# Requests for a pair's operands placed after the row of maxima and between the quarter refreshes on SyncE; one transfer for both copies' rows; the width table through a skewed view

## The chip, the cores and the metric

The kernel runs on one core of a Trainium2 chip. Its time is the device time of one execution in microseconds (us); the median of the runs is what counts.

## What is computed

Eight images of 32 x 32 tokens with 96 channels go through three residual blocks. Cut to what matters here:

```python
# layer 0: 6 heads of 16; rel_h, rel_w come from q and two tables of relative positions
attn = einsum('bqd,bkd->bqk', q * SCALE, k)
attn = attn.reshape(b*NH, h, w, h, w) + rel_h[:, :, :, :, None] + rel_w[:, :, :, None, :]
x = x + (softmax(attn.reshape(b*NH, hw, hw)) @ v -> heads joined) @ proj_w + proj_b     # input normed in groups
# layer 1: causal attention, 6 heads of 16
t = t + (softmax(where(causal, q @ k^T / 4, min)) @ v -> heads joined) @ w_proj          # input layer-normed
# feed-forward: 4 experts, the best 2 of each token weighted
t = t + sum over e of gate[e] * (gelu(LN(t) @ w1[e] + b1[e]) @ w2[e] + b2[e])
```

## The kernel before, in words

Five engines and the DMA queues run programs that are written out by hand; their order is the order of the code, and semaphores tie them together (`upto` gives the count that a stage of an item has to reach). An item is one image. The loop body is `attention(it, 1)` (layer 1 of item `it`), `attention(it, 0)` (layer 0 of the item after it) and `mix` (the experts of `it`, between them the norms and projections that the next item needs).

Each attention has three steps p = 0, 1, 2, one for a pair of heads, and each step runs over eight key tiles kt and the two heads hh of the pair. TensorE writes transposed scores to psT (L687 in layer 0, L690 in layer 1), ScalarE takes the exponential to probs (L1087), TensorE multiplies with the values (L709, L717). A row of negated maxima, one per query, is an extra row of the query operand, so it has to be there before the first scores of a pair. While pair p runs, TensorE computes plain scores for pair p + 1 (`max_scores`, L658) and VectorE reduces them (`maxima`, L1401); at kt = 6 the maxima are transposed (`transpose_max`, L668), ScalarE negates them (`neg_max`, L1042) and itself issues the transfer that lays them out as a row (L1048): `qr<-negb` in layer 1, `qs<-negr` in layer 0, where two copies of the query operand need it, so there are two transfers of 8 KB. In step p = 2 of layer 1 the same is done for pair 0 of the next layer 0 (called "lead").

The layer-0 operands of a pair are qs (128 rows, copies c = 0, 1) and ks, in slot p % 2. They are read back from DRAM by `load_pair(p)`, 17 transfers on SyncE's queue: for each copy two of 256 KB, two quarters of 64 KB and three of 128 KB, then three of 128 KB for ks: 2,432 KB in all. Only 8 of the 32 rows of relative height lie in a copy at a time (a quarter, for two key tiles): copy 0 has quarter 0 for kt 0 and 1 and gets quarter 2 for kt 4 and 5; copy 1 quarter 1, then quarter 3. ScalarE issues this refresh (L1085, two transfers of 64 KB) when it comes to the exponential of (kt = 1, hh = 1) or (kt = 3, hh = 1); TensorE waits for it at kt = 4 and 6 (`turn_in`). Before L1048 ScalarE waits in layer 0 for the whole pair (`pair_in`), since the row lies among the loaded rows.

SyncE's order: at the start of layer 1 `load_x`, then `first_pairs`, which is `load_pair(0)` and `load_pair(1)` of the next layer 0; then after each pair `gather` (eight transfers of 32 KB, when ScalarE has written `ot`). In layer 0: the token load x0 (L536), `load_pair(2)` when the scores of pair 0 are done (L482 on), `gather(0)`, `spill_levels` (query and key levels of the next item to DRAM, wait, and `qr` read back), `gather(1)`, `spill_wide` and its wait, `operands0` (qa, ka), `gather(2)`, then the slots of layer 1.

At the start of the program VectorE builds the table of relative widths with 32 instructions (L1312), then the other constants, then works on the relative terms (`rel_high` on ScalarE L1121, `rel_low` on VectorE L1530). `rel_high` waits at its first turn until all spills of queries and keys are in DRAM.

Of the kernel before, what the change touches and what calls it, by code (L numbers as in the profile page):

```python
# [15 lines left out]
NH, HD = 6, 16  # L16
# [104 lines left out]
def by_act(what):  # L121
# [37 lines left out]
    "negmax_in": {"attn1": 16 * (PAIRS - 1), "lead": 32, "attn0": 32 * (PAIRS - 1), "next_mix": 16},  # L159
# [98 lines left out]
def build(nc, x_tok, x_t, consts, hots, masks, w_qkv0, b_qkv0, w_p0, b_p0, rel_h, rel_w, w_qkv1, w_p1, gate_w, gate_b,  # L258
          w1, b1, w2, b2, out):
    with ExitStack() as ctx:  # L260
# [99 lines left out]
        mrow = sb("mrow", [P, 2, 2 * NT])  # L360
        negm = [sb("negr", [2 * NT, 2, P], F32R), sb("negb", [2 * NT, 2, P], BF16)]
# [13 lines left out]
        relr_w = probs[0:C, 1, :].rearrange("c (a b) -> c a b", a=WS)  # L375

# [38 lines left out]
        n_setup, n_ones = 28, 8  # L415
# [10 lines left out]
        def _(sp):  # L426
# [50 lines left out]

            def load_pair(p):

                heads, slot, done = slice(2 * p, 2 * p + 2), p % 2, pair_in[p % 2]  # L480
                for c in range(2):
                    sp.dma_start(qs_raw[W_HI:W_HI + WS, slot, c], scr_rel[R_W_HI:R_W_HI + WS, heads]).then_inc(done, 16)  # L482
                    sp.dma_start(qs_raw[W_LO:W_LO + WS, slot, c], scr_rel[R_W_LO:R_W_LO + WS, heads]).then_inc(done, 16)
                    for dst, src in quarter_rows(p, c, c):
                        sp.dma_start(dst, src).then_inc(done, 16)
                    for n, (q, _) in enumerate(S_PARTS):
                        a = QK_ROWS + n * HD
                        sp.dma_start(qs_raw[a:a + HD, slot, c], scr32_d[:, q, heads]).then_inc(done, 16)
                for n, (_, k) in enumerate(S_PARTS):
                    a = QK_ROWS + n * HD  # L490
                    sp.dma_start(ks_raw[a:a + HD, slot], scr32_d[:, k, heads]).then_inc(done, 16)
# [7 lines left out]
            def first_pairs(it, st):  # L499
# [3 lines left out]
                load_pair(0)  # L503
                load_pair(1)
# [19 lines left out]
            def attention1(it):  # L524
# [36 lines left out]
            spill_levels(None, "p_qkv0")  # L561
            spill_wide(None, "p_qkv0")
            operands0()
            relative(None, "p_rel")
            first_pairs(None, "p_rel")
# [18 lines left out]
        def _(pe):  # L584
# [79 lines left out]
            def transpose_max(it, layer, p):  # L664
# [3 lines left out]
                mm(psM[0:2 * NT, 0:P], mrow[:, p % 2, :], ident, is_transpose=True, start=True,  # L668
                   stop=True).then_inc(m_full, 1)

            def attention(it, layer):
# [55 lines left out]
                for p in range(PAIRS):  # L727
# [19 lines left out]

                    if layer == 0:
                        pe.wait_ge(negmax_in, upto("negmax_in", it, st, 32 * p))
                        pe.wait_ge(pair_in[p % 2], upto(("pair_a_in", "pair_b_in")[p % 2], it, st, PAIR_LOADS * (p // 2 + 1)))  # L750
                    else:
                        pe.wait_ge(negmax_in, upto("negmax_in", it, st, 16 * p))
# [168 lines left out]
            def first_rows(it, st):  # L921
# [5 lines left out]
                mm(o[0:2 * NT, 0:P], mrow[:, 0, :], ident, is_transpose=True, start=True, stop=True).then_inc(t_full, 1)  # L927
# [65 lines left out]
        def _(act):  # L993
# [44 lines left out]
            def neg_max(it, layer, p):  # L1038
# [3 lines left out]
                A(negm[layer][:, p % 2, :], psM[0:2 * NT, 0:P], ACT.Copy, scale=-1.0).then_inc(m_free, 1)  # L1042
# [19 lines left out]
            def attention(it, layer):  # L1062
# [232 lines left out]
        def _(dve):  # L1295
# [9 lines left out]
            def constants():  # L1305
# [368 lines left out]
```

## Time and profile before

| | |
|---|---|
| median of 3 runs | 2129.08 us (2126.45 to 2130.79) |
| profiled execution: its time, its span | 2129.47 us, 2127.6 us |
| granted TensorE clock, mean over the span | 0.915 of full speed |
| TensorE matmul, weight load | 1741.9 us (82%), 694.9 us (33%) |
| VectorE, ScalarE, GpSimd | 1222.2 us (57%), 1073.3 us (50%), 294.8 us (14%) |
| SP's queue (q1), ACT's queue (q10) | 180.18 MB, 6.79 MB |

TensorE is the busiest engine, but its share is an average over stages; what matters is what ends its idle times and at which point of an item they stand. Item 4 (layer 1 from 1012 us, layer 0 from 1092 us, mix from about 1182 us) is taken as the example below. Times in a timeline count from the start of the span. A bracket at the end of a timeline row is the idle time of the engine just before it and what ended it.

### The profile page before, as it was taken

The page shows a single profiled execution, that of the slowest core. Times are in us where ns is not written, and L with a number is a line of the kernel's source. Part 1 is how long each engine was busy: PE and PEld are TensorE (multiplying, and loading weights), DVE is VectorE, ACT ScalarE, POOL GpSimd, SP SyncE. Part 2 cuts the span into 40 slices and gives each one's busy share as a digit, 9 for nine tenths or more (in the row PEclk, how much of TensorE's full clock was granted, in tenths as well). Part 3 has the DMA queues.
Part 4 walks back from the last instruction along what each step waited for, and adds up shares of the span by engine and source line. Part 5 has one row for each costly group of instructions (what it writes and reads, how often), then busy time and mean ns, then how long its engine had stood idle before and what let it go on. Part 6 is the DMA issues. An engine that isn't in the chain of part 4 may idle for free.

```text
span 2127.6 us, 25037 instructions
## 1 busy us (share of the span) xinstructions
PE 1741.9 (82%) x8928; PEld 694.9 (33%) x8928; DVE 1222.2 (57%) x2526; ACT 1073.3 (50%) x1375; POOL 294.8 (14%) x191
## 2 busy tenths in 40 slices
PE   1578478898799968998798987999789987989858
PEld 0122222343233433343233432334322432324333
DVE  7753657446664657636674465646576365743631
ACT  0246335574456724575355743567345753566433
POOL 5112101301023100501023010321005010200000
PEclk7589579999899989999899998999899998999979
DMA  6756371636427291555606374372816446141200
GB/s 142 140 90 127 68 166 24 103 70 160 83 54 130 52 182 26 104 84 126 114 23 116 57 175 71 62 127 55 181 24 101 80 127 107 24 68 46 39 11 8
DMA packets 73744, 188.57 MB, mean 89 GB/s; under 512 B 23188, under 2 KB 24853, under 8 KB 66964
## 3 DMA queue, kind: packets, MB, share of 16 engines
q1 hardware_dynamic: 69780, 180.18, 44.3%
q10 hardware_dynamic: 3840, 6.79, 1.3%
q8 instruction: 71, 1.16, 0.3%
q14 instruction: 53, 0.43, 0.1%
HBM read 115.62 MB, written 58.20 MB: 82 GB/s over the span
## 4 chain that ended last, share of the span: by engine, by line
PE 53%; DVE 20%; DMA 12%; ACT 7%; issue 4%; SPq 2%; ACTq 1%; DVEq 0%
PE psS L658 11%; DVE mx L1401 8%; PE psOM L709 6%; PE psT L832 6%; PE psT L687 5%; PE psOM L717 5%; PE psS L846 5%; DMA qr<-negb 4%; PE psT L690 4%; DMA qs<-scr_rel 4%; DVE mrow L1503 3%; DMA qs<-negr 2%; DVE qs L1530 2%; ACT probs L1087 2%; PE psT L608 2%
## 5 line engine op out<-in xcount | busy, mean ns | idle before, releaser
L1087 ACT ACTIVATE probs<-psT 128x1024 f32<-128x1024 f32 (+7 forms) x768 | 623.6, 837 | 585.4 <-PE psT L687 250.8
L1401 DVE TENSOR_REDUCE mx<-psS 128x1 f32<-128x512 f32 (+3 forms) x1152 | 681.5, 640 | 390.4 <-PE psS L658 253.4
L687 PE MATMUL psT<-qs,ks 128*128 128x512 f32 x768 | 341.1, 515 | 44.0 <-DMA qs<-negr 16.0
L658 PE MATMUL psS<-ka,qa 128*128 128x512 bf16 x768 | 305.4, 407 | 45.1 <-DVE mx L1401 26.2
L690 PE MATMUL psT<-qr,kr 97*128 97x512 bf16 (+3 forms) x576 | 194.8, 367 | 64.8 <-DMA qr<-negb 63.8
L709 PE MATMUL psOM<-probs,v 128*32 128x512 f32 x1536 | 224.8, 608 | 11.6 <-ACT probs L1087 11.6
L832 PE MATMUL psT<-xf,w1s 97*128 97x512 f32 x384 | 187.4, 622 | 1.8 <-DVE mrow L1503 1.8
L658 PEld LDWEIGHTS psS<-ka,qa 128*128 128x128 bf16 x768 | 71.8, 97 | 344.4 <-DVE mx L1401 281.3
L687 PEld LDWEIGHTS psT<-qs,ks 128*128 128x128 f32 x768 | 141.0, 197 | 125.4 <-ACT probs L1087 48.0
L846 PE MATMUL psS<-probs,w2s 128*96 128x512 f32 x384 | 180.7, 596 | 0.8 <-ACT att L1146 0.8
L1530 DVE TENSOR_TENSOR qs<-psOM,qs 32x768 fp32r<-32x768 f32 x128 | 121.8, 952 | 95.2 <-ACT qs L1121 93.4
L717 PE MATMUL psOM<-probs,v 128*32 128x384 f32 (+3 forms) x1440 | 150.5, 444 | 20.4 <-ACT probs L1087 20.4
L658 PE MATMUL psS<-kr,qr 96*128 96x512 bf16 (+3 forms) x384 | 142.7, 384 | 22.9 <-DVE mx L1401 19.4
L1138 ACT ACTIVATE probs<-psT 128x1024 f32<-128x1024 f32 x96 | 98.3, 1024 | 115.8 <-PE psT L832 115.2
L1261 POOL TENSOR_TENSOR lb<-lb,il 96x1024 f32<-96x1024 f32 x7 | 16.6, 2371 | 785.3 <-ACT il L1111 785.3
L1503 DVE TENSOR_REDUCE mrow<-psT 128x1 f32<-128x128 f32 (+7 forms) x128 | 91.4, 753 | 46.9 <-PE psT L880 45.9
L1215 POOL TENSOR_TENSOR split<-au,split 96x1024 bf16<-96x1024 f32 x8 | 17.0, 2130 | 622.9 <-ACT split L1036 622.9
L832 PEld LDWEIGHTS psT<-xf,w1s 97*128 97x128 f32 x384 | 72.2, 197 | 85.3 <-issue 75.4
L690 PEld LDWEIGHTS psT<-qr,kr 97*128 97x128 bf16 x576 | 62.2, 108 | 101.0 <-DMA qr<-negb 68.4
L1512 DVE SCALAR_TENSOR_TENSOR x<-psOM,g,x 128x96 f32<-128x96 f32 x256 | 60.4, 308 | 60.0 <-PE psOM L864 60.0
L692 PE MATMUL psT<-mask_k,ident_b 128*128 128x128 bf16 x384 | 85.3, 232 | 0.0
L846 PEld LDWEIGHTS psS<-probs,w2s 128*96 128x96 f32 x384 | 58.1, 163 | 81.9 <-issue 72.8
(162 smaller groups left out, 1718.7 us busy)
## 6 DMA issues: line engine op xcount, KB each, us to landing
scr_rel<-qs SPq DMA_DIRECT2D x16, 1536.0 KB, 13.1
qs<-scr_rel SPq DMA_DIRECT2D x96, 256.0 KB
qs<-scr SPq DMA_DIRECT2D x144, 128.0 KB
scr<-split SPq DMA_DIRECT2D x24, 576.0 KB, 4.7
qr<-scr SPq DMA_DIRECT2D x48, 192.0 KB, 6.6
scr<-kr SPq DMA_DIRECT2D x24, 384.0 KB, 5.2
ks<-scr SPq DMA_DIRECT2D x72, 128.0 KB
qa<-scr SPq DMA_DIRECT2D x32, 192.0 KB, 5.4
```

The source lines that it names most:

```text
L658: last = mm(bank[:, 0:n], q[0:rows, h, t * P:(t + 1) * P], k[0:rows, h, kc * HALF:kc * HALF + n], start=True, stop=not diagonal)
L687: last = mm(o[:, a:b], ks[:, p % 2, hh, keys], qs[:, p % 2, kt // 2 % 2, hh, a:b], start=True, stop=True)
L690: last = mm(o[:, a:b], kr[:, h, keys], qr[:, h, a:b], start=True, stop=a != q0)
L709: last = mm(psO[j:j + 2 * HD, :], v[:, kt, p, hh * HD:(hh + 2) * HD], probs[:, (2 * kt + hh) % 4, c * HALF:(c + 1) * HALF], start=kt == 0, ...
L717: last = mm(psO[j:j + 2 * HD, first * P:HALF], v[:, kt, p, hh * HD:(hh + 2) * HD], every[:, c, first:], start=kt == 0, stop=kt == NT - NC + c)
L832: last = mm(o[:, c * HALF:(c + 1) * HALF], w1s[:, a:a + P], xf[:, c * HALF:(c + 1) * HALF], start=True, stop=True)
L846: last = mm(psS[0:C, c, :], w2s[:, n, :], hbuf[:, n % 4, c * HALF:(c + 1) * HALF], start=j == 0, stop=j == HJ - 1)
L1087: A(probs[:, n % 4, q0:T], psT[:, t_slot(ts, m), q0:T], ACT.Exp).then_inc(t_free, 1)
L1138: A(hbuf[:, n % 4, :], psT[:, t_slot(stage, fill), :], ACT.Gelu).then_inc(ta_free, 1)
L1401: V.reduce_max(mx[layer][:, p % 2, (h % 2) * NT + t, kc:kc + 1], psS[:, s_bank(st, fill), 0:max_cols(layer, t, kc)], AX).then_inc(s_free, 1)
L1503: V.reduce_max(mrow[:, 0, n:n + 1], psT[:, t_slot(st, fill), 0:cols], AX).then_inc(t_free, 1)
L1530: ins = V.tensor_tensor(rest[0], rest[1], lead[0].bitcast(F32), ALU.subtract)
```

## The change

- `first_pairs` is split: its waits (`spilled`) stay at the start of layer 1, the loads go. `load_pair(0)` now follows `gather(1, 0)` and a wait for the row of pair 1, `load_pair(1)` follows `gather(1, 1)` and a wait for the row of pair 2. In the prologue the order stays.
- `load_pair` is made of `load_copy(p, 0)`, `load_copy(p, 1)` and `load_keys(p)`. In layer 0, pair 2 is asked for in these parts: copy 0 when the scores of pair 0 are done, the keys and copy 1 during pair 1, after the one and the other refresh.
- The refreshes go from ScalarE's queue to SyncE's (`turn_quarter`, with a wait for the same scores).
- `spill_levels` is split: its waits and the reading back of qr (`levels_back`) now come after the refreshes of pair 2; `gather(0, 2)` comes ahead of `operands0`.
- Both copies' rows of maxima go in one transfer of 16 KB: the maxima are written twice side by side, 32 columns are transposed instead of 16.
- The table of widths: one broadcast copy (96 x 32 x 63) and one subtraction (96 x 32 x 32) through a view whose rows start one element further back each time.

```diff
+            def levels_back(it, st):
+
                 sp.wait_ge(spill_q, upto("spill_q", it, st, 16))
                 sp.wait_ge(spill_k, upto("spill_k", it, st, 16))
                 fill_slots(qr, scr_d, 0, Q_SLOTS, slice(0, NH), qr_in)
...
+            def turn_quarter(it, p, c):
+
+                st, n = att_t(0, (p * NT + 2 * c + 1) * 2 + 1)
+                sp.wait_ge(t_full, upto("t_full", it, st, n + 1))
+                for dst, src in quarter_rows(p, c, c + 2):
+                    sp.dma_start(dst, src).then_inc(turn_in[c], 16)
...
                 if next_lead(it):
-                    first_pairs(it - 1 if it else None, "mix")
+                    spilled(it - 1 if it else None, "mix")
                 for p in range(PAIRS):
                     gather(it, 1, p)
+                    if p + 1 < PAIRS and next_lead(it):
+                        sp.wait_ge(negmax_in, upto("negmax_in", it, "attn1", 16 * (p + 1)))
+                        load_pair(p)
 
             def attention0(it, row):
 
                 sp.wait_ge(t_free, upto("t_free", it, "attn0", 0))
                 sp.dma_start(x0[:, :, :], x_tok[row]).then_inc(x0_in, 16)
+                turn_quarter(it, 0, 0)
+                turn_quarter(it, 0, 1)
                 st, n = att_t(0, 2 * NT - 1)
                 sp.wait_ge(t_full, upto("t_full", it, st, n + 1))
-                load_pair(2)
+                load_copy(2, 0)
                 gather(it, 0, 0)
+                turn_quarter(it, 1, 0)
+                load_keys(2)
+                turn_quarter(it, 1, 1)
+                load_copy(2, 1)
                 if next_layer0(it):
                     spill_levels(it, "qkv0")
                 gather(it, 0, 1)
+                turn_quarter(it, 2, 0)
+                turn_quarter(it, 2, 1)
                 if next_layer0(it):
+                    levels_back(it, "qkv0")
                     sp.wait_ge(pair_in[0], upto("pair_a_in", it, "attn0", 2 * PAIR_LOADS))
                     spill_wide(it, "qkv0")
+                gather(it, 0, 2)
                 if next_layer0(it):
                     operands0()
-                gather(it, 0, 2)
...
-                rows = [qr[C:C + 1, 2 * p:2 * p + 2, :]] if layer else [qs_raw[MAX_ROW:MAX_ROW + 1, p % 2, c] for c in range(2)]
-                for row in rows:
-                    act.dma_start(row.rearrange("o h (t q) -> o (h t) q", q=P),
-                                  negm_raw[layer][:, p % 2, :]).then_inc(negmax_in, 16)
+                if layer:
+                    row = qr[C:C + 1, 2 * p:2 * p + 2, :].rearrange("o h (t q) -> o (h t) q", q=P)
+                else:
+                    row = qs_raw[MAX_ROW:MAX_ROW + 1, p % 2].rearrange("o c h (t q) -> o (c h t) q", q=P)
+                act.dma_start(row, negm_raw[layer][:, p % 2, :]).then_inc(negmax_in, 16)
...
-                            if layer == 0 and hh == 1 and kt in (1, 3):
-                                for dst, src in quarter_rows(p, kt // 2, kt // 2 + 2):
-                                    act.dma_start(dst, src).then_inc(turn_in[kt // 2], 16)
...
-                for r in range(WS):
-                    last = WIN - 1 - r
-                    ins = V.tensor_scalar(relr_w[:, r, :], relf_w[:, WS - 1 - r:last + 1], relf_w[:, last:last + 1], None,
-                                          ALU.subtract)
-                ready(ins)
+                ready(V.tensor_copy(straight, relf_w.unsqueeze(1).to_broadcast([C, WS, WIN])))
+                ready(V.tensor_tensor(relr_w, skewed, skewed[:, :, WS - 1:WS].to_broadcast([C, WS, WS]), ALU.subtract))
```

## Rows read from the trace of the kernel before

**Rows 1.** The page's part 4: the chain that ended last, by engine
```profile
PE 53%; DVE 20%; DMA 12%; ACT 7%; issue 4%; SPq 2%; ACTq 1%; DVEq 0%
```

**Rows 2.** The waits of PE, whole span: us in total, times, longest us
```profile
PE psT L690 <- DMA qr<-negb: 63.8, 16, 9.8
...
PE psT L687 <- DMA qs<-scr_rel: 12.4, 7, 3.0
```

**Rows 3.** Who waited for L1048 (us, times); then PE's waits in item 7's layer 1
```profile
  PE psT L690: 61.9, 15
...
PE psT L690 <- DMA qr<-negb: 0.2, 1, 0.2
```

**Rows 4.** Timeline, layer 1 of item 4, pair 0: SP's first load, ACT's row, TensorE's wait
```profile
1014.12 0.42 SPq L482 DMA_DIRECT2D qs<-scr_rel  x1
...
1032.83 0.52 ACTq L1048 DMA_DIRECT2D qr<-negb  x1
...
1042.04 0.61 PE L690 MATMUL psT<-qr,kr 97*128 97x512 bf16 x1 [7.69 <-DMA qr<-negb]
```

**Rows 5.** Busy time by window: length, PE, PEld, DVE, ACT, POOL, clock, DMA share, GB/s
```profile
1014.00:1042.00 28.00, 19.23 (x135) 7.80 (x133) 13.94 (x30) 10.11 (x17) 0.00 (x0) 0.81 1.04 188
...
1042.00:1050.00 8.00, 7.96 (x33) 3.82 (x37) 4.99 (x12) 4.37 (x5) 0.00 (x0) 0.50 0.46 82
...
1052.00:1060.00 8.00, 7.08 (x49) 2.48 (x47) 6.10 (x13) 3.78 (x7) 0.00 (x0) 1.00 0.03 7
```

**Rows 6.** Timeline, layer 1 of item 4, pair 2, to the first scores of layer 0
```profile
1070.73 0.39 PE L690 MATMUL psT<-qr,kr 97*128 97x512 bf16 x1 [0.24 <-DMA qr<-negb]
...
1073.90 0.51 SPq L449 DMA_DIRECT2D au<-ot  x1
...
1089.66 1.16 ACTq L1048 DMA_DIRECT2D qs<-negr  x2
...
1092.17 0.49 PE L687 MATMUL psT<-qs,ks 128*128 128x512 f32 x1 [0.34 <-DMA qs<-negr]
```

**Rows 7.** Chain that ended last, prologue: the first row of layer 0 (start, us, what)
```profile
105.59 11.11 DMA qs<-negr
```

**Rows 8.** Timeline, layer 0 of item 4, end of pair 0 to end of pair 1
```profile
1118.86 0.32 SPq L482 DMA_DIRECT2D qs<-scr_rel  x1
...
1131.29 0.65 ACTq L1085 DMA_DIRECT2D qs<-scr_rel  x2
...
1139.13 0.62 ACTq L1085 DMA_DIRECT2D qs<-scr_rel  x2
...
1142.56 0.50 PE L687 MATMUL psT<-qs,ks 128*128 128x512 f32 x1 [1.78 <-DMA qs<-scr_rel]
...
1154.17 1.16 ACTq L1048 DMA_DIRECT2D qs<-negr  x2
```

**Rows 9.** Timeline, layer 0 of item 4, pair 2: gather, refresh, scores of kt 4
```profile
1161.62 0.51 SPq L449 DMA_DIRECT2D au<-ot  x1
...
1166.53 0.59 SPq L450 DMA_DIRECT2D lb<-ot  x1
...
1168.33 1.65 ACTq L1085 DMA_DIRECT2D qs<-scr_rel  x2
...
1169.44 0.70 PE L687 MATMUL psT<-qs,ks 128*128 128x512 f32 x2 [0.34 <-ACT probs L1087]
1171.10 0.73 PE L687 MATMUL psT<-qs,ks 128*128 128x512 f32 x2 [0.95 <-ACT probs L1087]
```

**Rows 10.** Timeline of the prologue; last, a group by line (count, busy us, mean ns)
```profile
19.70 18.85 DVE L1312 TENSOR_SCALAR probs<-lb 96x32 f32<-96x32 f32 x32 [5.79 <-DMA il<-hots]
...
48.05 1.73 SPq L439 DMA_DIRECT2D qa<-scr  x4
...
57.88 0.80 ACT L1121 ACTIVATE qs<-psOM 32x768 fp32r<-32x768 f32 x1 [0.74 <-PE psOM L633]
...
L1412 DVE TENSOR_TENSOR lb<-lb,il 96x1024 f32<-96x1024 f32 x9 | 11.0, 1222 | 76.9 <-ACT il L1111 76.9
```

More of the change, by code:

```diff
@@ L158 @@
     "rowmax": {"attn1": PAIRS - 1, "lead": 1, "attn0": PAIRS - 1},
-    "negmax_in": {"attn1": 16 * (PAIRS - 1), "lead": 32, "attn0": 32 * (PAIRS - 1), "next_mix": 16},
+    "negmax_in": {"attn1": 16 * (PAIRS - 1), "lead": 16, "attn0": 16 * (PAIRS - 1), "next_mix": 16},
     "p_used": {s: ATT_FILLS for s in _ATT},
@@ L359, in build @@
         mx = [sb(f"mx{l}", [P, 2, 2 * NT, NC]) for l in (0, 1)]
-        mrow = sb("mrow", [P, 2, 2 * NT])
-        negm = [sb("negr", [2 * NT, 2, P], F32R), sb("negb", [2 * NT, 2, P], BF16)]
+        mrow = sb("mrow", [P, 2, 2, 2 * NT])
+        negm = [sb("negr", [4 * NT, 2, P], F32R), sb("negb", [2 * NT, 2, P], BF16)]
         negm_raw = [negm[0][:, :, :].bitcast(F32), negm[1]]
@@ L375, in build @@
         relr_w = probs[0:C, 1, :].rearrange("c (a b) -> c a b", a=WS)
+        copies = probs[0:C, 2:4, :].rearrange("c s t -> c (s t)")
+        straight = copies.rearrange("c (a b) -> c a b", b=WIN + 1)[:, :, 0:WIN]
+        skewed = copies[:, WS - 1:WS - 1 + WS * WIN].rearrange("c (a b) -> c a b", b=WIN)[:, :, 0:WS]
         gs6 = sb("gs6", [C, 2, 6])
@@ L414, in build @@
         first_loads = [(cst[:, :], consts), (wqkv[0][0:C, :], w_qkv0), (wqkv[0][C:C + 1, :], b_qkv0)]
-        n_setup, n_ones = 28, 8
+        n_setup, n_ones = 29, 8
         def quarter_rows(p, c, n):
@@ L476, in operands0, with load_copy, load_keys, load_pair @@
                 fill_slots(ka, scr_d, 1, K_SLOTS[:4], slice(0, NH), ab_in)
-            def load_pair(p):
+            def load_copy(p, c):
                 heads, slot, done = slice(2 * p, 2 * p + 2), p % 2, pair_in[p % 2]
[L481 to L488, printed above, removed]
+                sp.dma_start(qs_raw[W_HI:W_HI + WS, slot, c], scr_rel[R_W_HI:R_W_HI + WS, heads]).then_inc(done, 16)
+                sp.dma_start(qs_raw[W_LO:W_LO + WS, slot, c], scr_rel[R_W_LO:R_W_LO + WS, heads]).then_inc(done, 16)
+                for dst, src in quarter_rows(p, c, c):
+                    sp.dma_start(dst, src).then_inc(done, 16)
+                for n, (q, _) in enumerate(S_PARTS):
+                    a = QK_ROWS + n * HD
+                    sp.dma_start(qs_raw[a:a + HD, slot, c], scr32_d[:, q, heads]).then_inc(done, 16)
+            def load_keys(p):
                 for n, (_, k) in enumerate(S_PARTS):
                     a = QK_ROWS + n * HD
-                    sp.dma_start(ks_raw[a:a + HD, slot], scr32_d[:, k, heads]).then_inc(done, 16)
+                    sp.dma_start(ks_raw[a:a + HD, p % 2], scr32_d[:, k, 2 * p:2 * p + 2]).then_inc(pair_in[p % 2], 16)
+            def load_pair(p):
+                load_copy(p, 0)
+                load_copy(p, 1)
+                load_keys(p)
+            def turn_quarter(it, p, c):
[3 more added lines that the diff above has]
+                    sp.dma_start(dst, src).then_inc(turn_in[c], 16)
             def relative(it, st):
@@ L497, in relative, with spilled @@
                 sp.dma_start(scr_rel[:, 3:NH], rel_raw[:, 3:NH]).then_inc(spill_rel, 16)
-            def first_pairs(it, st):
+            def spilled(it, st):
                 sp.wait_ge(spill_rel, upto("spill_rel", it, st, 32))
                 sp.wait_ge(rel_lead_bf, upto("rel_lead_bf", it, st, NH))
-                load_pair(0)
-                load_pair(1)
             def slots1(it):
@@ L561, in _ @@
             spill_levels(None, "p_qkv0")
+            levels_back(None, "p_qkv0")
             spill_wide(None, "p_qkv0")
@@ L564, in _ @@
             relative(None, "p_rel")
-            first_pairs(None, "p_rel")
+            spilled(None, "p_rel")
+            load_pair(0)
+            load_pair(1)
             attention0(None, 0)
@@ L667, in transpose_max @@
                 pe.wait_ge(m_free, upto("m_free", it, ms, n))
-                mm(psM[0:2 * NT, 0:P], mrow[:, p % 2, :], ident, is_transpose=True, start=True,
+                rows = (4 - 2 * layer) * NT
+                mm(psM[0:rows, 0:P], mrow[:, p % 2].rearrange("p c r -> p (c r)")[:, 0:rows], ident, is_transpose=True, start=True,
                    stop=True).then_inc(m_full, 1)
@@ L746, in between @@
                         sent[0] = until
+                    pe.wait_ge(negmax_in, upto("negmax_in", it, st, 16 * p))
                     if layer == 0:
-                        pe.wait_ge(negmax_in, upto("negmax_in", it, st, 32 * p))
                         pe.wait_ge(pair_in[p % 2], upto(("pair_a_in", "pair_b_in")[p % 2], it, st, PAIR_LOADS * (p // 2 + 1)))
-                    else:
-                        pe.wait_ge(negmax_in, upto("negmax_in", it, st, 16 * p))
                     for kt in range(NT):
@@ L926, in first_rows @@
                 o = take_mixed(it, st, ("tmax", 0))
-                mm(o[0:2 * NT, 0:P], mrow[:, 0, :], ident, is_transpose=True, start=True, stop=True).then_inc(t_full, 1)
+                mm(o[0:2 * NT, 0:P], mrow[:, 0, 0, :], ident, is_transpose=True, start=True, stop=True).then_inc(t_full, 1)
             def group_means(it, st):
@@ L1041, in neg_max @@
                 act.wait_ge(negmax_in, upto("negmax_in", it, ms, 16 * max(p - 2, 0) if layer else 0))
-                A(negm[layer][:, p % 2, :], psM[0:2 * NT, 0:P], ACT.Copy, scale=-1.0).then_inc(m_free, 1)
+                A(negm[layer][:, p % 2, :], psM[0:(4 - 2 * layer) * NT, 0:P], ACT.Copy, scale=-1.0).then_inc(m_free, 1)
                 act.wait_ge(m_free, upto("m_free", it, ms, n + 1))
@@ L1405, in maxima @@
                         dve.wait_ge(m_full, upto("m_full", it, st, max(p - 1 - layer, 0)))
-                        V.tensor_tensor(mrow[:, p % 2, :], mx[layer][:, p % 2, :, 0], mx[layer][:, p % 2, :, 1],
-                                        ALU.max).then_inc(rowmax, 1)
+                        left, right = (mx[layer][:, p % 2, :, c].unsqueeze(1).to_broadcast([P, 2, 2 * NT]) for c in range(NC))
+                        V.tensor_tensor(mrow[:, p % 2], left, right, ALU.max).then_inc(rowmax, 1)
             def den(it, st):
@@ L1502, in first_maxima @@
                 dve.wait_ge(t_full, upto("t_full", it, st, fill + 1))
[L1503 removed]
+                V.reduce_max(mrow[:, 0, 0, n:n + 1], psT[:, t_slot(st, fill), 0:cols], AX).then_inc(t_free, 1)
             def expert_add(it, stage, x):
```

1 line of the change is left out of this document (removed).

## The prediction

> **What bounds the kernel now.** I read the chain that ended last first: TensorE carries 53% of it and transfers 12% [rows 1], so here it is worth asking which transfers TensorE sits and waits for. The waits of TensorE answer it: 63.8 us in 16 waits for `qr<-negb`, the row of maxima in layer 1, and 12.4 us in 7 waits for `qs<-scr_rel`, the quarter refresh of layer 0 [rows 2]. While TensorE waits at such a point nothing else goes on: VectorE's maxima and ScalarE's exponentials are fed by it. The reader should then separate long waits from short ones. The row issued at L1048 was waited for 15 times, 61.9 us together; the last item, which loads no pairs for a next one, waits 0.2 us [rows 3]. So the long ones are seven, one for each item with a next layer 0.
>
> The timeline shows why. SyncE asks for pairs 0 and 1 of the next layer 0 from 1014.12 on; ScalarE asks for the row at 1032.83; TensorE gets it at 1042.04 after 7.69 us of idleness [rows 4]. Up to that moment the transfer engines are busy without a gap (share 1.04, 188 GB/s), and afterwards they run on at 0.46 for some 8 us [rows 5]. The row stands behind 4.9 MB that nobody needs for 50 us. TensorE pays twice: for the next 8 us its granted clock is 0.50, the lower level (1.2 GHz), after it had stood idle, and in the window from 1052 it is 1.00 again [rows 5].
>
> **The change, step by step.** The sum is made against the profiled execution, 2129.5 us (span 2127.6, the rest lies around it); the median, 2129.1, is 0.4 us lower.
>
> *1. Row of pair 1 in layer 1.* The loads move behind it, so its queue is empty but for the store and `load_x`, asked for 18 us earlier. 15 waits of 61.9 us, eight of them short (0.24 us, as the one at 1070.73 [rows 6]; 8 x 0.24 = 1.9): seven long ones make 60.0 us. They shrink to 0.24 each: 60.0 - 1.7 = **-58.3**.
>
> *2. The clock after it.* In the 8 us at half clock VectorE did 4.99 us of work, in 8 us at full clock 6.10 [rows 5]. The same 4.99 would take 4.99 / 6.10 x 8 = 6.5 us: 1.5 us a stall, 10.5 for seven if all are like this one, 0 if VectorE sets the pace anyway. I take **-8**.
>
> *3. What is late next: the row of the lead pair.* `load_pair(1)` now goes out in pair 2 of layer 1, behind `gather(1, 1)`. Count from the start of that pair, 1070.73: the gather starts 3.2 us later and its eight issues take 5, so the load is asked for from +8.2. The row is asked for at +18.9 and used at +21.4 (1092.17) [rows 6]. A pair is 2,432 KB; at 188 GB/s that is 13.2 us, so the queue is full until +21.4, at the very time at which the row landed before. If the row passes, the cost is 0; if it waits for the whole queue and half of the 8 us tail that two pairs had [rows 5], it lands at about +26, 4.6 us late. I take 2 us, since the row of rows 4 came in when the full stretch ended and not after the tail: 7 x 2 = **+14** (0 to +32). The same for `load_pair(0)` and the row of pair 2: asked for from about +8 in a pair that lasts 28.7 us (1042.04 to 1070.73), it is through by +23, before the row goes out: 0 (to +4). The new wait of SyncE for the row of the next pair stands behind a gather that itself waits for that pair's first exponentials, so it is over when SyncE comes to it; `gather(1, 2)` and x0 queue behind, with 13 us to spare.
>
> *4. One transfer instead of two.* ScalarE spends 1.16 us on the two rows (1154.17 [rows 8]), one takes 0.52 [rows 4]: 0.64 us ahead of the last exponentials of a pair, on which TensorE's last values and the next pair wait. 16 such ends of pairs 0 and 1 in eight layers 0: **-10** (0 to -10). The lead row is in step 3. The wider transpose and reduction add columns to instructions that stand 40 times; nothing.
>
> *5. Refresh in pair 1 of layer 0.* Pair 2 is asked for at 1118.86, the refresh at 1131.29 behind it, and TensorE gets it at 1142.56, 1.78 us too late [rows 8]. Now only copy 0 (1,024 KB, 5.4 us at 188 GB/s) and a gather lie ahead of it; SyncE comes to it when the gather is issued, about 1131, so the refresh keeps its time of issue and lands 6 us before it is needed. The 12.4 us of [rows 2] go: **-12** (-8 to -18 with the clock). The cover of the moved part: copy 1 is now asked for after the refresh of 1139.13 and ScalarE needs it at 1154.17, less 3 us that the stage gets shorter [rows 8]: 11 us for 5.4 us of data. Behind copy 1 stand the spills (3 to 8 us later than before; TensorE first needs the read-back qr in the mix).
>
> *6. Refresh in pair 2.* Off ScalarE: at 1168.33 its issue takes 1.65 us beside SyncE's, and TensorE then waits 0.34 and 0.95 us for exponentials [rows 9]: -1 us in seven layers, -7 (0 to -9). On SyncE it stands behind `gather(0, 1)`, which goes from 1161.62 to 1167.1; two issues of 0.3 us and some 2 us of landing (the second lead row took 1.9 from 1090.3) put it at 1169.2 to 1169.8, and TensorE wants it at 1169.1 [rows 6, 9]. I take 0.5 us late, 8 x 0.5 = +4 (0 to +20 with a gather that starts later). Together **-3**. `levels_back` and `spill_wide` move behind it by some 5 us; `gather(0, 2)` waits for its own pair until 1182, which hides that.
>
> *7. The table.* 18.85 us of VectorE become one copy of 2016 and one subtraction of 1024 elements a row; 1024 elements took 1.22 us, so under 4 us [rows 10]. But ScalarE's first `rel_high` (57.88) also waits for the spills, and SyncE, which waits for the same, went on at 48.05 [rows 10]. The 15 us become 57.88 - 48.05 = **-10** (-8 to -10).
>
> Sum: -58.3 - 8 + 14 - 10 - 12 - 3 - 10 = -87.3; 2129.5 - 87.3 = 2042.2, on the median's footing about **2042 us**.
>
> **Rivals.**
> *The lead row passes.* Transfers on ScalarE's queue could be served between those of SyncE's. For it: by +18.9 all of `load_pair(1)` has been issued for 3 us, and what is left is mostly tail. Against it: rows 4, where the row was asked for 3 us after the last load and still took 9 us. Step 3 becomes 0: 2042 - 14 = 2028. The Trainium skill states such a rule ("DMA: Bandwidth & Descriptors", section "Queues, rings and completion order": each transfer engine goes round its queues packet by packet); by it the row of rows 4 should not have waited at all, so the trace speaks against it, and by it the sum would be the 2028 just worked out.
>
> *The wait only moves.* In the prologue the lead row is asked for behind two pairs and takes 11.11 us [rows 7] where it takes 1.9 in item 4: 9.2 us more. If one pair ahead does the same, step 3 is 7 x 9.2 = 64 instead of 14, and the clock falls there instead (step 2 gone): 2042 + 50 + 8 = 2100. Against it: half the bytes, asked for 11 us earlier.
>
> *The refresh of pair 2 is late by 2.5 us*, because SyncE is held in the gather: step 6 is +13 instead of -3: 2058.
>
> *Slower: ScalarE stuck behind copy 1.* ScalarE runs in order, and before the row of pair 2 it waits for all of the pair. What was asked for at 1131.29 behind pair 2 was usable at 1142.56, 23.7 us after the pair's first request [rows 8]. If copy 1, asked for at 1139.8, took as long, it would land 12.7 us after the 11 us it has; exponentials, values and the next pair stand still, in eight layers: +102, 2144. It turns the sign from 22 us of landing on (87 / 8 = 11 on top of the 11). Against it: 1 MB on a queue that is empty by then.
>
> *The row's wait has another cause* than the loads: steps 1, 2 and 3 fall away: 2042 + 52 = 2094. Item 7 speaks against it [rows 3].
>
> **How the numbers follow.** Forecast 0.47, lead row passes 0.22, late refresh 0.13, wait moves 0.12, stuck ScalarE 0.04, other cause 0.02. With the bounds of the steps the forecast itself runs from about 2018 to 2075. The range 2010 to 2085 takes in the first three with their bounds and leaves out the other 0.18. A measurement of this kernel can tell about 0.2% (4 us) from no change; only the stuck ScalarE lies on the slower side: slower 0.04, within 0.2% 0.02, faster 0.94.
>
> **What would show it.** Step 1: TensorE's waits for `qr<-negb` down from 63.8 to about 5 us. Step 2: the clock at 1.00 through the first 8 us of pair 1. Step 3: waits for `qs<-negr` at the start of layer 0, 2 us each, `load_pair(1)` issued 8 us into pair 2. Step 5: no wait for `qs<-scr_rel` in pair 1. Step 6: a wait for it at kt 4 of pair 2 of at most 1 us. Step 7: `rel_high` starting at 48. The forecast is wrong if the lead row waits 5 us or more, or if ScalarE stands before L1048 in pair 1 of layer 0.

## The result, and the profile after

The changed kernel takes 2110.3 us (median of 8 runs, 2106.1 to 2117.1) where the kernel before took 2128.2 us (median of 8 as well): a ratio of 0.9919, 95% interval 0.9900 to 0.9937. It is faster, as forecast, but by 18 us instead of 87, and 2110 lies above the range. What came is the rival that had 0.12: the wait moved to the lead pair's row. Lines have moved: L687 is now L722, L690 is L725, L658 is L692, L1048 is L1083, L1085 is L512 (on SyncE), L482 is L487, L1087 is L1118.

The page's chain by engine, after, against [rows 1]:

```profile
PE 56%; DVE 21%; DMA 9%; ACT 6%; issue 4%; SPq 3%; another core or an unknown queue 2%; ACTq 0%; DVEq 0%
```

Transfers fell from 12 to 9% of the chain, no more. (The 2% of an unknown queue stand where 61 of L692's 768 matmul records are missing from this trace.) TensorE's waits for transfers, after, against [rows 2] (us in total, times, longest):

```profile
PE psT L722 <- DMA qs<-negr: 65.7, 8, 14.2
...
PE psT L725 <- DMA qr<-negb: 20.7, 16, 4.2
...
PE psT L722 <- DMA qs<-scr_rel: 17.2, 8, 3.2
```

The row of layer 1 went from 63.8 to 20.7 us. But the row of layer 0 takes 65.7 us in 8 waits, one of them the prologue's 14.2, so (65.7 - 14.2) / 7 = 7.4 us in each item. Before, that row stood in the same view as:

```profile
PE psT L687 <- DMA qs<-negr: 16.0, 11, 12.6
```

The sums of both rows are 86.4 us after and 79.8 us before (63.8 and 16.0).

Where the time went shows best stage by stage. A stage here runs from the timeline's start of one pair's first score matmul to that of the next pair; the means are over the seven items that have a next layer 0, in us. The last line runs from the first to the last score matmul of the pair only. The kernels e1 to g1 are the experiments below. Each column is one profiled execution.

```
stage               before  after    e4    e1    e2    f3    e3    f1    g1
layer 1, pair 0      27.18  18.85 27.42 18.91 18.80 18.64 18.65 18.79 27.02
layer 1, pair 1      27.76  27.40 28.03 28.00 27.71 28.34 27.76 25.45 27.63
layer 1, pair 2      21.43  29.53 21.16 22.58 23.01 26.00 30.12 21.18 21.16
layer 0, pair 0      29.67  30.10 28.84 34.58 28.58 30.05 30.03 29.00 29.22
layer 0, pair 1      34.52  31.45 31.44 32.88 31.43 31.46 31.50 31.45 35.03
layer 0, pair 2      20.06  21.53 22.01 21.68 21.62 21.05 19.59 19.60 20.24
```

Pair 0 of layer 1 gave 8.33 x 7 = 58.3 us and pair 2 took 8.10 x 7 = 56.7 of them back. What the kernel kept is pair 1 of layer 0, 3.07 x 7 = 21.5 us. By the six lines together the seven items gained 12.3 us of the 18.6 by which the two spans (2127.6 and 2109.0) differ; the rest lies outside them, in the mixes and at the program's start.

The item of [rows 4 to 9], timeline after, from pair 2 of layer 1 to the first scores of layer 0 (a bracket is the idle time before, and what ended it):

```profile
1056.81 0.61 PE L725 MATMUL psT<-qr,kr 97*128 97x512 bf16 x1 [1.67 <-DMA qr<-negb]
...
1066.32 1.83 SPq L487 DMA_DIRECT2D qs<-scr_rel  x1
...
1073.58 1.36 SPq L499 DMA_DIRECT2D ks<-scr  x3
...
1077.03 0.51 ACTq L1083 DMA_DIRECT2D qs<-negr  x1
...
1079.40 0.51 SPq L452 DMA_DIRECT2D au<-ot  x1
...
1084.38 0.58 SPq L558 DMA_DIRECT2D x<-x_tok  x1
...
1087.68 1.67 PE L722 MATMUL psT<-qs,ks 128*128 128x512 f32 x2 [8.94 <-DMA qs<-negr]
```

`load_pair(1)` goes out from 1066.32, the lead row at 1077.03, and TensorE has it 10.6 us later, after 8.94 us of idleness. Busy time by window of the same stretch, after (columns as in [rows 5]: length, PE, PEld, DVE, ACT, POOL, clock, DMA share, GB/s):

```profile
1070.00:1075.00 5.00, 4.18 (x31) 1.28 (x29) 4.66 (x8) 2.18 (x4) 0.00 (x0) 1.00 1.03 152
1075.00:1080.00 5.00, 2.95 (x34) 1.29 (x30) 1.19 (x3) 2.08 (x6) 0.00 (x0) 1.00 1.05 184
1080.00:1085.00 5.00, 0.00 (x0) 0.00 (x0) 0.00 (x0) 0.00 (x0) 0.00 (x0) 0.56 0.88 113
1085.00:1088.00 3.00, 0.32 (x1) 0.29 (x1) 0.00 (x0) 0.00 (x0) 0.00 (x0) 0.50 0.92 156
1088.00:1092.00 4.00, 3.81 (x9) 1.38 (x9) 2.66 (x5) 1.94 (x2) 0.00 (x0) 0.64 0.09 29
```

The transfer engines are at 0.88 to 1.05 of their time until TensorE has its row, and from 1080 to 1085 no compute engine does anything. The granted clock falls to the lower level in the idle time, and it is still below the upper one when layer 0 begins: what [rows 5] showed at the start of pair 1 now stands here.

### The profile page after: what moved, and what is told of

It reads as the page before. It is cut to its first block, busy times and chain, and to the rows that moved or that the text cites. A ratio compares the mean times of both kernels' runs of the same rounds, so it can differ in the third digit from the quotient of the medians.

```text
span 2109.0 us, 24922 instructions
## 1 busy us (share of the span) xinstructions
PE 1729.6 (82%) x8867; PEld 693.9 (33%) x8928; DVE 1221.8 (58%) x2496; ACT 1071.8 (51%) x1375; POOL 298.9 (14%) x191
## 4 chain that ended last, share of the span: by engine, by line
PE 56%; DVE 21%; DMA 9%; ACT 6%; issue 4%; SPq 3%; another core or an unknown queue 2%; ACTq 0%; DVEq 0%
PE psS L692 12%; DVE mx L1429 9%; PE psOM L744 7%; PE psT L722 6%; PE psT L865 5%; PE psOM L752 5%; PE psS L879 4%; PE psT L725 4%; DMA qs<-negr 4%; DVE mrow L1531 3%; DVE qs L1558 2%; PE psT L642 2%; DMA qr<-negb 2%; DVE x L1540 1%
## 5 line engine op out<-in xcount | busy, mean ns | idle before, releaser
L1118 ACT ACTIVATE probs<-psT 128x1024 f32<-128x1024 f32 (+7 forms) x768 | 622.5, 836 | 578.0 <-PE psT L722 299.9
L722 PE MATMUL psT<-qs,ks 128*128 128x512 f32 x768 | 351.8, 533 | 90.8 <-DMA qs<-negr 65.7
L692 PE MATMUL psS<-ka,qa 128*128 128x512 bf16 x707 | 292.7, 421 | 36.3 <-DVE mx L1429 16.7
L725 PE MATMUL psT<-qr,kr 97*128 97x512 bf16 (+3 forms) x576 | 194.3, 366 | 23.0 <-DMA qr<-negb 20.7
L722 PEld LDWEIGHTS psT<-qs,ks 128*128 128x128 f32 x768 | 147.1, 205 | 170.3 <-DMA qs<-negr 67.9
L692 PEld LDWEIGHTS psS<-ka,qa 128*128 128x128 bf16 x768 | 74.3, 100 | 347.9 <-DVE mx L1429 281.9
L865 PE MATMUL psT<-xf,w1s 97*128 97x512 f32 x384 | 182.2, 607 | 1.8 <-DVE mrow L1531 1.8
L692 PE MATMUL psS<-kr,qr 96*128 96x512 bf16 (+3 forms) x384 | 135.1, 363 | 25.1 <-DVE mx L1429 20.8
L910 PE MATMUL psT<-kr,qr 96*128 96x512 bf16 (+1 forms) x192 | 53.5, 352 | 35.4 <-DVE mrow L1531 14.8
## 6 DMA issues: line engine op xcount, KB each, us to landing
scr<-kr SPq DMA_DIRECT2D x24, 384.0 KB, 11.5
```

The costliest lines, as they stand in the source:

```text
L692: last = mm(bank[:, 0:n], q[0:rows, h, t * P:(t + 1) * P], k[0:rows, h, kc * HALF:kc * HALF + n], start=True, stop=not diagonal)
L722: last = mm(o[:, a:b], ks[:, p % 2, hh, keys], qs[:, p % 2, kt // 2 % 2, hh, a:b], start=True, stop=True)
L725: last = mm(o[:, a:b], kr[:, h, keys], qr[:, h, a:b], start=True, stop=a != q0)
L865: last = mm(o[:, c * HALF:(c + 1) * HALF], w1s[:, a:a + P], xf[:, c * HALF:(c + 1) * HALF], start=True, stop=True)
L1118: A(probs[:, n % 4, q0:T], psT[:, t_slot(ts, m), q0:T], ACT.Exp).then_inc(t_free, 1)
```

## Experiments

**e4: the loads back where they were.** All of the change but its first part.

```diff
                     spilled(it - 1 if it else None, "mix")
+                    load_pair(0)
+                    load_pair(1)
                 for p in range(PAIRS):
                     gather(it, 1, p)
-                    if p + 1 < PAIRS and next_lead(it):
-                        sp.wait_ge(negmax_in, upto("negmax_in", it, "attn1", 16 * (p + 1)))
-                        load_pair(p)
```

> The changed kernel with both pairs' loads put back to the start of layer 1 as before; all else of the change stays. Theory: moving the loads only moved the wait from the row of pair 1 (pair 0 back to 27 us) to the lead row (pair 2 back to 21.4 us), so it was worth next to nothing, and this kernel takes 2105 to 2115, as the changed one; what the change gained is in pair 1 of layer 0 (some 3 us an item) and in the prologue. Rival: the move of the loads gained what the change gained, and the rest nothing: then this kernel takes about 2128.

2107.2 us, ratio 0.9909 (0.9877 to 0.9941), not to be told from the changed kernel. The move of the loads, the part with the largest term, is worth nothing as it was made; TensorE's wait for `qr<-negb` is back, and that for `qs<-negr` is down to (16.9 - 12.2) / 7 = 0.7 us an item outside the prologue:

```profile
PE psT L724 <- DMA qr<-negb: 64.2, 17, 10.0
...
PE psT L721 <- DMA qs<-negr: 16.9, 8, 12.2
```

**e1: all of pair 1 behind the lead row.** Its three lots go out between the refreshes in pair 0 of layer 0.

```diff
-                    if p + 1 < PAIRS and next_lead(it):
+                    if p == 0 and next_lead(it):
...
                 turn_quarter(it, 0, 0)
+                if it is not None:
+                    load_copy(1, 0)
+                    load_keys(1)
                 turn_quarter(it, 0, 1)
+                if it is not None:
+                    load_copy(1, 1)
```

> The changed kernel, but pair 1 of the next layer 0 is asked for behind the lead row: copy 0 and the keys after the first refresh of layer 0, copy 1 after the second. Theory A, the lead row waits for what SyncE's queue still has to move ahead of it: with nothing ahead, pair 2 of layer 1 goes from some 29.5 us back to the 21.4 it took before, the seven waits of some 7 us for the row go to 0.3; about 50 us less than the changed kernel, 2055 to 2065. Theory B, the single transfer of 32 rows into one partition is itself slow: pair 2 stays at 29 us and the time at 2110. In both, pair 0 of layer 0 may grow by 1 to 3 us if copy 1 comes late for the row of pair 1.

2107.4 us, ratio 0.9898 (0.9859 to 0.9937): Theory A came out for the stage, but not for the time. The lead pair falls from 29.53 to 22.58 us, so it was `load_pair(1)` that the lead row stood behind. But pair 0 of layer 0 rises from 30.10 to 34.58 and pair 1 from 31.45 to 32.88, which takes most of it back. The timeline of e1 there:

```profile
1091.84 0.31 SPq L487 DMA_DIRECT2D qs<-scr_rel  x1
...
1105.83 0.56 ACTq L1088 DMA_DIRECT2D qs<-negr  x1
...
1106.48 1.94 ACT L1123 ACTIVATE probs<-psT 128x1024 f32<-128x1024 f32 x2 [2.94 <-DMA qs<-scr]
1107.56 2.84 PE L749 MATMUL psOM<-probs,v 128*32 128x512 f32 x8 [2.38 <-ACT probs L1123]
...
1111.93 0.49 PE L727 MATMUL psT<-qs,ks 128*128 128x512 f32 x1 [1.53 <-DMA qs<-negr]
```

Copy 1, asked for at 1091.84, is there 14 us later; ScalarE stands 2.94 us ahead of its row, TensorE 2.38 us for the exponentials behind it, and then 1.53 us for the row itself. The wait has moved a third time, and in the form that the prediction had called ScalarE stuck behind copy 1, only one pair earlier.

**e2: half of pair 1 ahead of the lead row.** Copy 0 (1,024 KB) stays in pair 2 of layer 1; keys and copy 1 go out in layer 0, as in e1.

```diff
-                        load_pair(p)
+                        if p == 0:
+                            load_pair(0)
+                        else:
+                            load_copy(1, 0)
...
                 turn_quarter(it, 0, 0)
+                if it is not None:
+                    load_keys(1)
                 turn_quarter(it, 0, 1)
+                if it is not None:
+                    load_copy(1, 1)
```

> The changed kernel, but only copy 0 of pair 1 (1,024 KB of 2,432) is asked for ahead of the lead row, in pair 2 of layer 1; the keys come after the first refresh of layer 0, copy 1 after the second. Theory A (the row waits until the queue ahead of it is through): 1,024 KB are through about 8 us after the request, 3 us before the row is asked for, so pair 2 takes 21.4 to 22 us and the time is that of the kernel with all of it behind, or up to 5 us less. Rival: any load in that pair holds the row up in proportion to its bytes; then pair 2 takes about 25 us and the time is about 2080.

2057.3 us, ratio 0.9676 (0.9636 to 0.9716): some 50 us less than the changed kernel and near to the forecast of 2042. The lead pair takes 23.01 us instead of 29.53, and pair 0 of layer 0 28.58, without the price that e1 paid there. Timeline of e2 at the lead row:

```profile
1051.19 0.51 ACTq L1090 DMA_DIRECT2D qs<-negr  x1
...
1053.44 0.51 PE L729 MATMUL psT<-qs,ks 128*128 128x512 f32 x1 [0.53 <-DMA qs<-negr]
```

With 1,024 KB asked for from 1040.59 on, the row takes 2.2 us; with 2,432 KB it took 10.6. By the trace's records of single pieces of a transfer, the last piece of those 1,024 KB goes 1.2 us before the row is asked for. So the mechanism of the forecast was sound, and its size was not.

**f3: the same requests with two quarters fewer.** Both copies' quarters of pair 1 (four transfers of 8 rows, 256 KB of 2,432) move into layer 0; everything else stays ahead of the lead row. The third argument of `load_copy` says whether the quarters go with it; `load_quarter` asks for them alone.

```diff
-                        load_pair(p)
+                        load_copy(p, 0, p == 0)
+                        load_copy(p, 1, p == 0)
+                        load_keys(p)
...
                 turn_quarter(it, 0, 0)
+                if it is not None:
+                    load_quarter(1, 0)
+                    load_quarter(1, 1)
```

> The changed kernel, but the four quarter transfers of pair 1 (64 KB each, 8 rows each, 256 KB of its 2,432) are asked for in layer 0, after the first refresh, no longer ahead of the lead row. Theory A, the row waits for bytes: 10% less at 150 GB/s is 1.7 us, so pair 2 of layer 1 takes 27.8 us instead of 29.5 and the time falls by some 12 us. Theory B, the 8-row transfers load only half of the transfer engines and it is their longer backlog that holds the second half of the row: then the row comes 3.5 us earlier or more, pair 2 takes 26 us or less and the time falls by 25 us.

2086.7 us, ratio 0.9792 (0.9761 to 0.9824). TensorE's waits in f3:

```profile
PE psT L732 <- DMA qs<-negr: 40.6, 8, 12.6
```

(40.6 - 12.6) / 7 = 4.0 us an item instead of 7.4, and the lead pair is 3.5 us shorter. At some 150 GB/s (the mean of the windows above until the row came), 262,144 bytes are 1.7 us. So these four cost about twice what their bytes do. The Trainium skill ("DMA: Bandwidth & Descriptors", section "Why a DMA increments its semaphore by 16 and not by 1") says that a transfer is spread over the largest number of engines, up to 16, that divides the outer dimension of both its sides; for 8 rows that would be 8 of them. The 3.5 us agree. How the row itself moves agrees too. It goes as 48 small pieces on ScalarE's queue (q10). In the changed kernel half of them move in the window 1081.4:1083, none in 1083:1084.8, and the other half in 1084.8:1086.2; in f3 all 48 move in 1066.5:1069.2 (pieces, MB, share of 16 engines):

```profile
q10 hardware_dynamic: 24, 0.01, 4.7%
...
q10 hardware_dynamic: 24, 0.01, 4.2%
...
q10 hardware_dynamic: 48, 0.02, 5.6%
```

In all seven items of the changed kernel the second half starts 2.5 to 3.5 us after the first, in f3 0.4 to 0.8 us. The records do not name the engine of a piece, and the same bytes in transfers of 16 rows were not run. That it was half of the engines fits, but is not shown.

**e3: the refresh ahead of the gather.** In pair 2 of layer 0.

```diff
-                gather(it, 0, 1)
                 turn_quarter(it, 2, 0)
+                gather(it, 0, 1)
                 turn_quarter(it, 2, 1)
```

> The changed kernel, with one line moved: SyncE issues the first refresh of pair 2 ahead of the gather of pair 1, no longer behind it. Theory: the 17 us of waiting for the refresh in pair 2 (eight waits of about 2 us) come from the 5 us that SyncE spends on the gather; they go to under 3 us together, and the time falls by 8 to 14 us to about 2098. Rival: the refresh is late because its landing is slow or because TensorE has become faster there, not by the place in the queue; then the waits stay at 1.5 us or more each and the time at 2110.

2099.7 us, ratio 0.9880 (0.9843 to 0.9916). Timeline of the changed kernel, pair 2 of layer 0:

```profile
1152.51 0.51 SPq L452 DMA_DIRECT2D au<-ot  x1
...
1153.70 1.67 SPq L452 DMA_DIRECT2D au<-ot  x1
...
1158.58 1.49 SPq L512 DMA_DIRECT2D qs<-scr_rel  x4
...
1162.45 2.02 PE L722 MATMUL psT<-qs,ks 128*128 128x512 f32 x4 [2.46 <-DMA qs<-scr_rel]
```

and of e3:

```profile
1155.19 0.61 SPq L512 DMA_DIRECT2D qs<-scr_rel  x2
1155.85 0.51 SPq L452 DMA_DIRECT2D au<-ot  x1
...
1162.71 1.56 PE L722 MATMUL psT<-qs,ks 128*128 128x512 f32 x4 [0.34 <-ACT probs L1118]
```

Behind the gather the refresh goes out at 1158.58 and TensorE loses 2.46 us; ahead of it the wait is gone, and the scores of the pair take 19.59 instead of 21.53 us: 1.94 x 7 = 13.6 us. The medians differ by 10.6 us as expected, but the intervals of the two ratios overlap.

**e6: the constants after GpSimd.** VectorE waits with the table until GpSimd has done its first spills.

```diff
                 dve.wait_ge(first_in, 16 * len(first_loads))
+                dve.wait_ge(wide3, upto("wide3", None, "p_qkv0", 2))
```

> The changed kernel, but VectorE's constants, the table among them, wait until GpSimd has made the first operand parts. In the changed kernel the first eight of these instructions took 1.8 to 3.0 us each, small ones of 63 columns too, while GpSimd was at work; the same ones took 0.2 to 1.3 us before. Theory A, it is GpSimd's work beside them that stretches them: after it, the small ones take 0.2 to 0.3 us, those of 1024 columns 0.7 to 1.3, the copy of 2016 columns about 2 and the subtraction 1.2; the constants start 16 us later and the relative terms some 2 to 5 us later than in the changed kernel. Theory B, their operands or the view make them slow: the times stay as they were and the relative terms start 15 us later.

2121.7 us in one run. The question was how long the instructions take by themselves. Timeline of the prologue, VectorE and GpSimd, in the changed kernel:

```profile
19.82 1.21 DVE L1341 COPY probs<-lb 96x2016 f32<-96x2016 f32 x1 [5.92 <-DMA il<-hots]
21.07 3.03 DVE L1342 TENSOR_TENSOR probs<-probs 96x1024 f32<-96x1024 f32 x1
...
25.08 2.19 DVE L1345 SCALAR_TENSOR_TENSOR lb<-lb,cst 96x63 f32<-96x63 bf16 x1
...
38.73 6.33 DVE L1351 CAST ka<-au 64x1024 bf16<-64x1024 f32 x6
...
20.03 2.98 POOL L1266 TENSOR_TENSOR xnt<-kr,split 96x1024 f32<-96x1024 f32 x1
23.08 1.92 POOL L1267 CAST split<-xnt 96x1024 bf16<-96x1024 f32 x1
```

and in e6:

```profile
36.91 1.21 DVE L1342 COPY probs<-lb 96x2016 f32<-96x2016 f32 x1 [22.99 <-POOL kr L1276]
38.15 1.22 DVE L1343 TENSOR_TENSOR probs<-probs 96x1024 f32<-96x1024 f32 x1
...
39.64 0.28 DVE L1346 SCALAR_TENSOR_TENSOR lb<-lb,cst 96x63 f32<-96x63 bf16 x1
...
44.58 4.29 DVE L1352 CAST ka<-au 64x1024 bf16<-64x1024 f32 x6
...
20.04 2.12 POOL L1266 TENSOR_TENSOR xnt<-kr,split 96x1024 f32<-96x1024 f32 x1
22.23 1.03 POOL L1267 CAST split<-xnt 96x1024 bf16<-96x1024 f32 x1
```

Alone, the subtraction takes 1.22 us and an addition of 63 elements 0.28; beside GpSimd they take 3.03 and 2.19, and GpSimd's own steps grow from 2.12 to 2.98 and from 1.03 to 1.92. The table's instructions took 4.3 us instead of 18.9. But the eight behind them took 14.6 us where they had taken 5.1, and the casts 6.3 where they had taken 4.3: of 14.6 us saved, 11.5 were spent by instructions that moved up beside GpSimd's work.

**g1: only the one transfer for both rows,** in the kernel before.

```diff
-                rows = [qr[C:C + 1, 2 * p:2 * p + 2, :]] if layer else [qs_raw[MAX_ROW:MAX_ROW + 1, p % 2, c] for c in range(2)]
+                row = qs_raw[MAX_ROW:MAX_ROW + 1, p % 2].rearrange("o c h (t q) -> o (c h t) q", q=P)   # layer 0
```

> The kernel before with one part of the change alone: both copies' rows of maxima go in one transfer (the maxima written twice side by side, 32 columns transposed), everything else as before. Step 4's theory: the 0.64 us of ScalarE ahead of the last exponentials are on the path, so each end of pairs 0 and 1 of layer 0 comes some 0.6 us earlier: pair 1 of layer 0 and pair 0 of layer 0 each 0.6 us shorter, 16 ends, about -10 us, ratio about 0.995. Rival: ScalarE's issue lies beside TensorE's own work, and the wider transpose and reduction cost as much as the saved issue: no stage shorter by more than 0.2 us, ratio within 0.002 of 1; then the 3 us by which pair 1 of layer 0 got shorter in the changed kernel all belong to the refresh (step 5).

2122.0 us, ratio 0.9967 (0.9948 to 0.9986), some 7 us (3 to 11): between the two expectations, with 10 us inside the interval. Its profiled execution, 2130.4 us, is the slowest of its 12 runs, so differences of half a microsecond in its stages prove little. Pair 2 of layer 1 is 0.27 us shorter and pair 0 of layer 0 0.45. Pair 1 of layer 0 is not shorter but 0.5 longer, and TensorE's waits in g1 fit that:

```profile
PE psT L688 <- DMA qs<-scr_rel: 17.3, 8, 3.5
```

against 12.4 us in [rows 2]: TensorE came earlier to a refresh that still stood behind pair 2's load. So the 3.07 us that the changed kernel gains in that pair go with the refresh and its queue; nothing in g1 gives them to the one transfer.

**f1: three lots, every row on an empty queue.** Copy 0 of pair 0 at the start of layer 1; its copy 1 and keys behind the row of pair 1; copy 0 of pair 1 behind the row of pair 2; its keys and copy 1 between the refreshes of layer 0, in the prologue too; and the edit of e3.

```diff
                     spilled(it - 1 if it else None, "mix")
+                    load_copy(0, 0)
                 for p in range(PAIRS):
...
-                        load_pair(p)
+                        if p == 0:
+                            load_copy(0, 1)
+                            load_keys(0)
+                        else:
+                            load_copy(1, 0)
...
                 turn_quarter(it, 0, 0)
+                if it is None:
+                    load_copy(1, 0)
+                load_keys(1)
                 turn_quarter(it, 0, 1)
+                load_copy(1, 1)
```

> The changed kernel with the loads spread so that each row of maxima finds the queue empty: copy 0 of pair 0 at the start of layer 1, copy 1 and keys of pair 0 in pair 1, copy 0 of pair 1 in pair 2, its keys and copy 1 after the first and second refresh of layer 0 (in the prologue all of pair 1 there); the first refresh of pair 2 ahead of the gather. Theory (a row costs what SyncE's queue still holds when it is asked for, 1.4 MB being through in some 11 us after a gather): the waits for the row of pair 2 of layer 1, some 2.8 us each in the kernel with half of pair 1 ahead, go to 0.3 (-18 us), the prologue's 12 us wait to 1 (-11), the refresh's 17 to 2 (-4 to -10): about 2024 from 2057, pair 1 of layer 1 from 27.6 to 25 us. Rival: pair 1 is as long as it is for another reason (VectorE's 32 maxima and the group statistics); then it stays at 27 us and the time is about 2040.

2014.5 us, ratio 0.9458 (0.9424 to 0.9491): faster than both kernels, by 118 us against a kernel before that took 2132.9 on this experiment's chip. Transfers carry 4% of its chain. TensorE's waits in f1:

```profile
PE psT L730 <- DMA qs<-negr: 10.4, 9, 3.2
...
PE psT L733 <- DMA qr<-negb: 5.8, 16, 2.1
```

Both rows together cost 16.2 us where they cost 79.8 before and 86.4 after the change. Pair 1 of layer 1, which hardly moved in any other kernel, falls from 27.40 to 25.45 us: it was still held by the row of pair 2 behind `load_pair(0)`, and the rival, that VectorE paces it, falls. f1 makes several edits at once; the stages tell them apart, and the largest gain is in the lead pair (29.53 to 21.18).

## Why the prediction was wrong

*Step 1, the row of pair 1, was right:* -58.3 forecast, -58.3 measured by the stage (27.18 to 18.85, seven times).

*Step 3 failed, by its size.* It put +14 where +56.7 came. The order of events was as foreseen: the load from 9.5 us into pair 2 (8.2 forecast), the row asked for at 20.2 (18.9). What it had wrong is how long the load holds the row: it let 2,432 KB through in 13.2 us and added 2 us. The trace's records of single pieces tell the load's apart by their size (4,096 and 8,192 bytes). From first to last they take 15.7 to 17.6 us in the seven items, which is 142 to 158 GB/s, and the first goes 1.2 to 2.5 us after the request. In item 4 the last one is through at 1085.85, 19.5 us after the request, and the last piece of the row goes at 1085.91; the two lie within 0.1 us of each other in every one of the seven items. Then it is 1.8 us more until TensorE starts. So the row waits for the whole load. Two readings were wrong. The first is the rate. 188 GB/s came from one window of 28 us [rows 5]. Cut into pieces of 4 us, the same stretch of the kernel before reads:

```profile
1014.00:1018.00 4.00, 3.78 (x15) 1.60 (x14) 2.60 (x5) 1.17 (x2) 0.00 (x0) 0.50 1.04 291
1018.00:1022.00 4.00, 4.00 (x21) 1.34 (x19) 2.36 (x4) 2.71 (x3) 0.00 (x0) 0.64 1.04 146
...
1026.00:1030.00 4.00, 3.88 (x34) 1.55 (x33) 3.00 (x7) 2.31 (x5) 0.00 (x0) 1.00 1.05 148
```

The 291 GB/s of the first four are not of the pairs alone (the store and `load_x` precede them); behind them the rate is at times below 150. The second is that a mean rate is not what the row sees. The row's first half goes at 1081.5, with some 300 KB of the load still to move, and its second half 3.4 us later with the load's last pieces (f3). What SyncE was asked for behind the row is not needed to explain the wait. In item 6 x0 is asked for only after TensorE has its row:

```profile
1569.88 0.51 ACTq L1083 DMA_DIRECT2D qs<-negr  x1
...
1576.48 0.79 PE L722 MATMUL psT<-qs,ks 128*128 128x512 f32 x1 [5.08 <-DMA qs<-negr]
...
1577.04 0.58 SPq L558 DMA_DIRECT2D x<-x_tok  x1
```

The pieces of `gather(1, 2)` move beside the load's last ones; what they add is not shown. Nor is it shown why the row of [rows 4], whose pieces go at 1039.84 to 1040.2, passed the tail that the pairs still had, and the lead row did not. The row of pair 2 was put at 0 (to +4) and cost more as well: of the 20.7 us of `qr<-negb`, eight short waits make 1.9, the first row of the first layer 1 makes 2.2, and 16.5 are left, 2.4 in each of seven items.

*Step 2* forecast -8 for the clock. It is up in pair 1 (1.00 from 1030 to 1038 in the changed kernel), but the stage gained only 0.36 x 7 = 2.5 us, while the row of pair 2 is waited for at its end, and the clock falls at the start of layer 0 instead. In f1, where neither row is waited for long, the stage takes 25.45 us.

*Step 4* said -10; g1 gives -7 (-11 to -3). *Step 5* said -12: the wait for `qs<-scr_rel` in pair 1 is gone, and pair 1 of layer 0 gave 21.5 us. With both copies' rows in one transfer but the old refresh (g1), the stage was 35.03, so the refresh and ScalarE's two issues that went with it made 3.58 x 7 = 25. That the kernel got faster at all is owed mostly to this stage and not to the largest terms: steps 1 and 3 together came to -1.6.

*Step 6* said -3, with 0.5 us of lateness. The refresh is late by 17.2 / 8 = 2.15 us and the scores of the pair grew from 20.06 to 21.53: +10. It is the rival of the late refresh, which came beside the other one: the gather's issues took from 1152.51 to 1158.53, one of them 1.67 us, and TensorE had the refresh some 3.9 us after its issue, not 2.

*Step 7* said -10. `rel_high` starts at 54.89 instead of 57.88 [rows 10], -3.0. The sum had taken the table's instructions at the duration of the same size elsewhere and had not asked what GpSimd does at that time.

*The rivals.* "The wait only moves" had priced the lead row at 9.2 us, and 2100 in all: the row cost 7.4 and the stage 8.1. Steps 6 and 7 came out 13 and 7 us worse than forecast and pair 1 of layer 0 some 5 us better, which brings it near to 2110. "The lead row passes" falls. The Trainium skill's rule behind it ("DMA: Bandwidth & Descriptors", section "Queues, rings and completion order") lets each engine go round its queues packet by packet; a row on ScalarE's queue that takes 10.6 us while SyncE's is full, and 2.2 when it is not (e2), speaks against reading it as a short wait. How many pieces of a transfer make up such a packet no run here shows, so the forecast's "should not have waited at all" was more than the rule says, and in what order the engines take the two queues stays open. "ScalarE stuck behind copy 1" did not come in the changed kernel, but e1 brought it about.

## What to carry to other kernels

A load that is moved out of the way of one small transfer is put in the way of the next: list every small transfer that somebody waits for, and give each lot a size that is through before the next of them is asked for (here 1,024 to 1,408 KB between two rows; 2,432 KB were too much). Take the rate of a drain from a stretch that holds the same kind of transfers alone, and ask when its last piece is through and not when the mean rate says so: the lead row went with it. And an instruction that is moved to another time has another neighbour: look at what runs beside it there before its duration is taken from elsewhere.

## What was not expected of the hardware

In these rows VectorE and GpSimd wait for each other's whole instructions. In the prologue of the changed kernel GpSimd's L1266 starts at 20.03, 1.0 us before VectorE's copy ends (21.03), and takes 0.86 us longer than in e6; VectorE's subtraction starts at 21.07, 1.94 us before L1266 ends (23.01), and takes 1.81 us longer than in e6. The Trainium skill ("SBUF — State Buffer", section "Who interferes with whom") states it as an exclusive lock for VectorE's copies in a two-port mode and, against a GpSimd instruction that reads SBUF, for its instructions with two SBUF inputs; the rows agree. The table's 32 instructions before the change did not slow GpSimd: its L1235 and L1236 took 2.12 and 1.03 us there, as in e6.

Four transfers of 8 rows, 256 KB together, held a row up for 3.5 us where the mean rate gives 1.7 (f3).

And an issue on SyncE, mostly 0.3 to 0.6 us, takes up to 2.0 us at times (1066.32, 1153.70 above). In the changed kernel's trace each of the 23 issues of over 1 us has a transfer of the kind "instruction" beside it, 16 KB in 22 cases and 8 KB in one; at 1153.6:1155.1 (transfers, MB, share):

```profile
q8 instruction: 1, 0.02, 5.2%
```

That this transfer holds the issue is not tested. It is not what makes the refresh of pair 2 late: in three of the eight layers 0 no issue of the gather took more than 0.6 us, and TensorE still waited 1.3 to 3.2 us.
